# An attention turn in which the values of two turns back come ahead of the scores

## The reference, cut to what matters

```
x = x + attention(layernorm(x))           # x: 8 sequences of 256 tokens, 256 wide
x = x + experts(layernorm(x))             # 8 experts, each token to the best 2

attention:  q = x wq, k = x wk, v = x wv  # 32 query heads, 8 key/value heads, 64 wide
            q, k = rope(q), rope(k)
            s = q k^T / 8, causal mask;  p = softmax(s);  o = p v;  return o wo
```

## Time and profile before

| | |
|---|---|
| device time, median of 3 runs | 798.24 us (796.76 to 799.06) |
| the profiled execution: its own time | 795.58 us |
| its span, first to last instruction | 793.8 us |
| mean granted TensorE clock over the span | 0.989 of full speed |
| busy: PE / PE weight loads / DVE / ACT / POOL | 747.8 / 640.4 / 560.9 / 505.5 / 428.3 us |
| scores of the first turn, and of the last, start at | 21.55 and 553.52 us |

### The profile page before, as it was taken

How to read it: one execution, slowest core, us unless ns; L and a number is a source line. 1 busy time by engine, 2 the same in 40 slices (tenths; PEclk the granted TensorE clock), 3 DMA queues, 4 the chain that set the end, 5 groups by cost and what they waited for, 6 DMA issues and landing times.

```text
span 793.8 us, 19659 instructions
## 1 busy us (share of the span) xinstructions
PE 747.8 (94%) x6080; PEld 640.4 (81%) x6080; DVE 560.9 (71%) x2166; ACT 505.5 (64%) x1562; POOL 428.3 (54%) x673
## 2 busy tenths in 40 slices
PE   5799999999999999999999999999799999999993
PEld 5678888888888888888888888877577777888883
DVE  6887677667666757766775785888756656777772
ACT  2678877776776777677777667768554433555551
POOL 1466665656656556465565546555424544566552
PEclk9899999999999999999999999999999999999997
DMA  8343031212211211221221212123973232222330
GB/s 251 97 125 117 29 89 48 68 41 68 74 35 55 61 62 47 63 67 39 71 68 35 61 41 68 41 67 109 374 266 51 43 53 41 50 42 48 55 54 5
DMA packets 52854, 61.07 MB, mean 77 GB/s; under 512 B 10544, under 2 KB 45616, under 8 KB 52752
## 3 DMA queue, kind: packets, MB, share of 16 engines
q1 hardware_dynamic: 44816, 50.07, 20.6%
q0 software_dynamic: 7488, 9.36, 7.0%
q10 hardware_dynamic: 448, 0.39, 0.3%
HBM read 26.21 MB, written 9.32 MB: 45 GB/s over the span
## 4 chain that ended last, share of the span: by engine, by line
PE 72%; DVE 13%; issue 5%; DMA 4%; ACT 4%; POOL 1%; SPq 1%; POOLq 0%; DVEq 0%; ACTq 0%
PE h L1669 12%; PE attn_out L541 10%; PE projected L387 9%; PE probsT L501 9%; PE scores L488 8%; PE heads_out L520 5%; PE yb L1711 4%; PE projected L408 3%; PE heads_out L523 2%; PE yb L1694 2%; PE projected L365 2%; PE tg L1682 2%; DMA xs<-xn_rows,from_token 2%; DVE masked L759 1%; DVE masked L761 1%
## 5 line engine op out<-in xcount | busy, mean ns | idle before, releaser
L1011 POOL TENSOR_SCALAR probs<-exps,inv_sums 128x128 f32<-128x128 f32 x256 | 96.5, 377 | 215.2 <-DVE inv_sums L767 165.0
L626 ACT COPY pT<-probsT 128x384 f32<-128x384 f32 x256 | 121.7, 475 | 79.2 <-PE probsT L501 79.1
L617 ACT ACTIVATE exps<-masked,neg_max 128x128 f32<-128x128 f32 x256 | 103.1, 403 | 57.8 <-DVE neg_max L761 57.4
L501 PE MATMUL probsT<-identity,probs 128*128 128x128 f32 x768 | 130.2, 279 | 5.3 <-ACT pT L626 5.2
L619 ACT ACTIVATE exps<-masked,neg_max 128x256 f32<-128x256 f32 x256 | 127.3, 497 | 0.0
L1012 POOL TENSOR_SCALAR probs<-exps,inv_sums 128x256 f32<-128x256 f32 x256 | 124.7, 487 | 0.0
L1972 POOL DMA_INDIRECT out<-y,to_token x39 | 69.3, 1777 | 94.7 <-DVE y L1888 48.9
L387 PE MATMUL projected<-xT_hi,w 128*128 128x256 f32 x488 | 106.4, 298 | 2.5 <-DVE k_sin L749 1.6
L1669 PE MATMUL h<-experts_w,xsT_hi 128*128 x312 | 104.6, 416 | 4.0 <-DVE experts_w L1559 2.0
L488 PE MATMUL scores<-kT,qT 64*128 64x128 f32 (+1 forms) x1024 | 103.1, 340 | 5.6 <-DMA qT<-rotated 4.1
L761 DVE CUSTOM_DVE_ANT_0 masked<-scores,tables 128x256 f32<-128x256 f32 x256 | 107.5, 420 | 0.2 <-issue 0.2
(11 more groups left out here) (208 smaller groups left out, 1683.1 us busy)
## 6 DMA issues: line engine op xcount, KB each, us to landing
qT<-rotated SPq DMA_DIRECT2D x254, 64.0 KB, 2.2
experts_w<-w_in SPq DMA_DIRECT2D x16, 512.0 KB, 7.6
kT<-k_cos SPq DMA_DIRECT2D x62, 128.0 KB, 3.4
raw<-w_attn SPq DMA_DIRECT2D x20, 256.0 KB, 3.0
experts_w_out<-w_out SPq DMA_DIRECT2D x8, 512.0 KB, 9.1
out<-x_all SPq DMA_DIRECT2D x8, 256.0 KB, 2.4
xn_rows<-raw SPq DMA_DIRECT2D x8, 256.0 KB, 2.7
x_all<-x SPq DMA_DIRECT2D x1, 1792.0 KB, 11.2
```

Source lines behind the costliest of these rows:

```text
L501: mm = nc.tensor.transpose(p_bank[:, at:at + P], probs[:, h, at:at + P], ident[:, :])
L617: nc.scalar.activation(exps[:, h, 0:P], masked[:, h, 0:P], ACT.Exp, bias=neg_max[:, h, 0:1], scale=-1.0, accum_out=sums[:, h, 0:1])
L626: nc.scalar.copy(pT[:, n % 2, h, :], p_bank[:, 0:3 * P]).then_inc(pT_done, 1)
L1011: nc.gpsimd.tensor_scalar(probs[:, h, 0:P], exps[:, h, 0:P], inv_sums[:, h, 0:1], 1.0, ALU.mult, ALU.mult)
```

## The change

In PE's turn the call of `values` for two turns back moves from behind the scores to ahead of them. The first two turns of all have no values, so 62 turns are changed. The two `values` after the last turn stay as they are. No instruction is added or removed, and no wait, and no other engine's list changes.

```
         def turn(b, g):
 
-            scores(b, g)
             if past(b, g, 2):
                 values(*back(b, g, 2))
+            scores(b, g)
             if past(b, g, 1):
                 prob_transposes(*back(b, g, 1), 1)
             whole = projects(b, g)[0] in ("x", "k", "v", "r")
```

## The result

The changed kernel takes 847.74 us (median of 6 runs, 846.71 to 850.78); the kernel before, on the same chip, 797.5 us. The quotient of the two medians is 1.0630; the ratio estimated from the runs is 1.0647, with a 95% interval of 1.0626 to 1.0669. So the swap costs 50 us, and the forecast of 848 us holds.

A forecast was written before the change was run, and what follows sets the result against it. TensorE was taken as the bound, with 72% of the chain. Delays of 36.2 us (sequences 1 to 6), 4.5 (sequence 0), 1.65 and 7.5 (last) sum to 50 us, on a 798.24 us median: 848 us, range 828 to 864.

The forecast's parts named there:

- The values can't be used earlier: ACT: `oT_hi` queues behind exponentials delayed to T+3.28, T being the start of the turn's first matmul.
- The copy of head 1 holds up the transposes of head 2: Plain turns g=0, g=7: ACT's copy ends at T+5.12, transposes start at T+5.26 instead of T+4.29, 0.97 us late.
- In whole turns the rope is what is late: g=1, g=6: DVE's later rope delays TensorE's other projection to T+7.46 from T+6.78, 0.68 us.
- One sign: Expected in the changed profile: in g=1, 2 and 6, TensorE idle before L365, L387 or L408, ended by DVE.
- the distances of g=4: Offsets from E, start of head 0's exponentials: `oT_hi` E+0.89, head 1 copy ends E+1.84, `oT_lo` E+2.18, rope E+4.12.
- g=2 waits for the keys: g=2: the q projection waits for DVE's `k_sin`, starting at T+4.51 instead of T+3.26, 1.25 us late.
- g=4 and g=5 were late before and pay less: DVE's first piece, already late there, moves from T+2.37 and T+1.83 to T+2.60: 0.23 and 0.77 us.
- The switches between kinds of matmul cost nothing more: TensorE: some 0.06 us a switch, three a turn, 62 turns; bounded at 11 us either way, taken as zero.
- The sums: Sequence 0: 4.5 us; sequences 1 to 6: 36.2; last sequence: 1.65 for g=0 and g=1 plus 7.5 for the others.
- The whole delay in every turn: Rival 1: later divisions or ropes bind everywhere, 62 turns times 1.45 = 90 us, 888 us; chance 0.06.
- the other side: Rival 3: not slower; plain turns wait for nothing and switches give back up to 11 us, 787 us; chance 0.04.
- the second rival: TensorE's clock falls to half in one turn in four, 125 us more, 973 us with the sum; chance 0.04.

The follow-up runs named there:

- the ACT experiment: On the changed kernel, ACT takes `oT_hi` (out_hi) ahead of the exponentials of head 0; 832.81 us, ratio to the kernel before 1.0441.
- the layer norm edit: DVE's layer norm steps ahead of the last inverses in g=3 and g=4, sequences 1 to 6: 791.54 us on the kernel before, 847.38 on the changed one.
- cutting the values: On the kernel before, only the first pair of heads' values goes ahead of the scores, the second stays behind; 813.87 us, ratio 1.0197.

## Why the prediction was right, point by point

- *The values can't be used earlier.* Shown: `oT_hi` stands behind the exponentials without a wait for TensorE, and takes its place ahead of them only if ACT's list is changed too. The exponentials start at T+3.29, forecast T+3.28.
- *The copy of head 1 holds up the transposes of head 2.* T+5.26 in g=7, as forecast. The experiment on ACT's list moved both together, the copy by 0.50 and the transposes by 0.49.
- *In whole turns the rope is what is late.* T+7.46 in g=6, as forecast, 0.05 after the end of the rope; and in the ACT experiment the projection is late with the rope though the transposes of head 2 are on time. One sign was named wrongly: in these turns of sequences 1 to 5 TensorE shows no idle time before L365 and L408. Most of the 0.69 is lost earlier, at the transposes of head 2 (0.49, for ACT), and the rest, which the rope adds, is covered by the last transposes, which run on. That the rope is late by way of `oT_lo` and the exponentials of head 1 is argued from the distances of g=4; the ACT experiment, which moves all of these, gives 0.46 of the 0.69 back.
- *g=2 waits for the keys.* T+4.51 as forecast, after 1.00 of idling that DVE ended, and the wait is gone when the keys are roped first.
- *g=4 and g=5 were late before and pay less.* 0.20 and 0.79; in the total, the swap in g=4 alone can't be told from no change (by turns it is 0.19), and the layer norm edit is worth 6 us before and nothing that can be told from zero after.
- *The switches between kinds of matmul cost nothing more.* Values and scores together take 2.97 in the new order and 2.96 in the old. The term is right at nothing, but its bound of 11 us was not earned: cutting the values showed that one more entry into them, with its waits, costs 0.15, not 0.06. At that price three switches in each of 62 turns would have been 28 us.
- *The sums.* Sequence 0: 4.2 for 4.5. Sequences 1 to 6: 37.1 for 36.2. The last: 9.9 for 9.15, and that excess has another cause, g=7, told below. That the total came out within 1 us is in part luck: 0.75 and 1.25 a turn for the first and the last sequence were means of wide bounds (measured, 0.03 to 1.27 in sequence 0 and 0.84 to 2.37 in the last), and in sequence 6 misses of up to 1.0 a turn cancelled. The spans differ by 54.2, more than the 50.2 of the medians: in these two executions the first two turns, which are the same in both kernels, differ by 1.3 (17.4 and 18.7), and the stretch after the attention by another 1.3.
- *The rivals.* The whole delay in every turn is refuted by g=3 and g=4, the other side by all. The clock stayed at 1.00 in sequences 1 to 6, but the second rival has a small part in the last. The step that led past it, that all new waits stay below the 1.53 which had left the clock alone, did not hold there: g=6 and g=7 of the last sequence each have one of 1.75.

## What to carry to other kernels

When engines work through lists written by hand, a piece that is moved ahead helps only if the one who uses it can take it earlier; look at what stands in front of it in the user's list. What is pushed back by it costs only beyond the slack of each place, so read a turn that is late already: its distances price the change for all the others. And where an engine idles for an input, see whether later work of its list could stand there: that gave 0.7% here with no work removed.

## What the runs showed of the hardware that had not been expected

Apart from the first 40 us and the last 15, in which it is low for a while in both kernels, the clock fell once in the kernel after, in the last turn of the attention, g=7 of the last sequence. Windows of the kernel after (length, busy PE, PEld, DVE, ACT, POOL, then clock, DMA share, GB/s):

```profile
600.00:602.00 2.00, 1.57 (x12) 1.34 (x13) 1.90 (x10) 1.05 (x6) 0.82 (x2) 1.00 0.72 188
...
608.00:610.00 2.00, 0.52 (x3) 0.31 (x3) 2.00 (x9) 1.98 (x8) 1.21 (x2) 0.98 1.09 246
610.00:612.00 2.00, 1.30 (x6) 1.31 (x7) 2.00 (x8) 0.49 (x3) 1.12 (x3) 0.50 0.98 309
...
614.00:616.00 2.00, 2.00 (x31) 1.52 (x31) 1.04 (x5) 1.64 (x8) 0.82 (x2) 0.50 1.03 422
616.00:618.00 2.00, 2.00 (x19) 1.29 (x15) 0.59 (x4) 1.97 (x4) 0.82 (x2) 0.82 1.03 418
```

TensorE had waited 1.75 for ACT until 609.27 and 0.91 for DVE until 610.70, and was busy 0.52 of the two microseconds from 608. From 610 to 616 the clock was at 1.2 GHz, and g=7 took 11.61 us. But a wait of the same length one turn earlier left the clock at 1.00 (the first window above). Timeline of TensorE in g=6:

```profile
599.94 0.52 PE L501 MATMUL probsT<-identity,probs 128*128 128x128 f32 x3 [1.75 <-ACT pT L626]
```

The changed kernel with the layer norm edit has the same lists there and the same two waits in g=7, 1.75 and 0.91, and kept 2.4 GHz; windows of that kernel:

```profile
610.00:612.00 2.00, 1.09 (x10) 0.86 (x9) 2.00 (x8) 1.00 (x5) 1.63 (x3) 1.00 0.93 291
...
614.00:616.00 2.00, 1.84 (x37) 1.56 (x39) 1.13 (x7) 1.74 (x8) 1.22 (x3) 1.00 1.03 418
```

Its g=7 took 10.70, so the fall cost 0.9 us, which more than covers the excess of the last sequence. In the other sequences the new waits, up to 1.07, never brought the clock down. The kernels with out_hi first and with rope_k first also fell in their last sequence, to 0.50 in the windows from 586 to 592 and from 608 to 612. Why some executions fell and the one with the layer norm edit did not, and what sets the wait in g=7 apart from that in g=6, stays open. The Trainium skill (TensorE: Matmul & The Clock Gate, section "A second HAM failure mode: psum-queue depth-cycling") says that frequent short pauses between groups of matmuls can make the clock swing between its two levels; the trace agrees at most in this one place, where it fell once after two pauses, and shows no swing in the turns of sequences 1 to 6, which have a pause each.
